# Cross attention and a 32-expert feed-forward layer: the routing weights' way from one row each to 64 rows

## The chip, the cores and the metric

The kernel runs on one core of a Trainium2 chip. The metric is the device time of one execution in microseconds (us). The core has a matrix engine (PE, TensorE), a vector engine (DVE, VectorE), a scalar engine (ACT, ScalarE), GpSimd (POOL) and SyncE (SP), which here only issues DMAs. Each engine runs its own list of instructions in order and waits on semaphores. PE writes to PSUM (8 banks of 128 partitions x 512 float32); DVE and ACT read and write PSUM and SBUF; POOL and the DMAs reach SBUF but not PSUM.

## What is computed

Four batches of 256 tokens, 128 channels. One layer of self and cross attention, then a feed-forward layer (FFN) with a shared expert and 32 routed experts, of which each token uses the best 8. The part that the change touches:

```python
x = hidden_states.reshape(T, h)                       # T = 1024 tokens, h = 128
aff = jax.nn.sigmoid(jnp.dot(x, Wr) + br)             # 32 experts
top_v, top_i = jax.lax.top_k(aff, 8)
top_w = top_v / (jnp.sum(top_v, axis=-1, keepdims=True) + 1e-09)
w_full = jnp.zeros((T, 32)).at[jnp.arange(T)[:, None], top_i].set(top_w)
gate = silu(jnp.einsum('th,ehi->eti', x, Wg) + bg[:, None, :])   # i = 64
up = jnp.einsum('th,ehi->eti', x, Wu) + bu[:, None, :]
down = jnp.einsum('eti,eih->eth', gate * up, Wd) + bd[:, None, :]
routed = jnp.einsum('te,eth->th', w_full, down)
```

## The kernel before

**Attention.** The attention runs in 16 steps (4 batches x 4 groups of 4 heads). In step i, PE computes score tiles (`natural`, `scores`), the probabilities times the values of step i-1 (`attend_self`, `attend_context`, into PSUM bank 6, `B_OUT`), and transposes the output of step i-2 (`turn_out`, into bank 7, `B_MISC`). DVE divides that output by its denominator (`normalize`). Bank 7 is also used by the "tail" of each batch: `y_turn`, `project`, `x2_turn`, `router`, `route_turn`. `take_misc` makes PE wait, before it writes bank 7 again, for whoever reads it. The tails of batches 0 and 1 stand in the steps 6 to 15, those of batches 2 and 3 beside the first items of the FFN (`pe_beside`, `act_beside`, `v_beside`).

**FFN.** Tokens lie along the free dimension in two chunks of 512. Two experts of 64 inner rows make one unit of 128 rows; unit 16 is the shared expert. An item is one unit and one chunk: `WORK` has 34 items, 32 of them routed. The items 0 to 11 are chunk 0, item 12 is the first of chunk 1. Float32 precision is kept by splitting each operand in a rounded upper half (`_hi`) and the rest (`_lo`), so that each product is three matmuls (`product3`). For each routed item:

1. PE: `project_gate` (3 matmuls, bank 0 or 1), the up projection (3 matmuls, bank 2 or 3), and `spread_routes` (1 matmul, L1687, bank 4 or 5): it multiplies the transposed routing weights `routeT` with a 0/1 matrix `spread`, so that the weight of each of the two experts stands in 64 rows.
2. ACT: silu of the gate into `gate` in SBUF (L925).
3. DVE: `gated` = (up + bias) * gate (L1300), then `hid` = gated * the spread weights in PSUM (L1312).
4. ACT rounds `hid` to `hid_hi` (L934); the lower half `hid_lo` is made by POOL for the items 0 to 11 and 31 (L707) and by DVE for the others (L974).
5. PE: the down projection of item n-2 (3 matmuls), added up in bank 6 or 7.

`spread` is made by POOL (`make_spread`) and copied by ACT during the attention steps. The weights of the units are loaded by SP (`load_unit`, three DMAs of 64 KB each, a ring of 6 slots) and split by ACT (L814) and POOL (L638). SP's list is: all loads up to unit 16, then the three stores of the result.

The routing weights of batch b are made by DVE (`router`, `top`, `weights`), transposed by PE (`route_turn`, L1611) and copied to `routeT` by ACT (L834). Chunk c needs the batches 2c and 2c+1.

Of the kernel before, what the change touches and what calls it, by code (L numbers as in the profile page):

```python
# [6 lines left out]
F32R = mybir.dt.float32r  # L7
# [25 lines left out]
SPREADS = 4  # L33
SPREAD_UNITS = 4
# [33 lines left out]
B_GATE, B_UP, B_WIDE = 0, 2, 4  # L68
# [8 lines left out]
def build(nc, x, ctx, w, out):  # L77

    with ExitStack() as stack:
# [17 lines left out]
        spread = sb("spread", [P, PAIRS, P], F32R)  # L97
# [49 lines left out]
        top = sb("top", [P, 2, TOP])  # L147
# [4 lines left out]
        routeT = sb("routeT", [P, TOKENS], F32R)  # L152


        with ExitStack() as attention:
# [8 lines left out]
            spread_f = sb("spread_f", [P, SPREAD_UNITS, P], until=attention)  # L164
# [26 lines left out]
        in_ffn = [sem(f"in_ffn{k}") for k in range(SLOTS)]  # L191
        placed_k = [[sem(f"placed_k{k}_{g}") for g in range(GROUPS)] for k in range(2)]
# [14 lines left out]
        have_spread = sem("have_spread")  # L207
# [54 lines left out]
        spread_copied = sem("spread_copied")  # L262
# [34 lines left out]
        m_wide = sem("m_wide")  # L297
# [26 lines left out]
        for b in range(BATCH - 2):  # L324
            for n, name in enumerate(TAIL):
                tail_at.setdefault(4 * b + 6 + n, []).append((name, b))
            between_at[4 * b + 8] = [("norm", b)]
        late_at[11] = [("route_turn", 0)]
# [11 lines left out]
                     (5, "C"): [("route_turn", 2), ("x2_turn", 3)],  # L340
                     (6, "C"): [("router", 3)],
                     (LEAD - 2, "B"): [("route_turn", 3)]}
# [3 lines left out]
                      (5, "C"): [("route_turn", 2), ("x2_turn", 3)],  # L346
                      (7, "B"): [("router", 3)],
                      (LEAD - 2, "B"): [("route_turn", 3)]}
# [7 lines left out]
                    (6, "A"): [("x2_turn", 3)],  # L356
                    (6, "C"): [("router", 3)],
                    (7, "C"): [("top", 3)],
                    (8, "C"): [("weights", 3)]}
# [5 lines left out]
        POOL_LO = [*range(LEAD), LAST_ITEM - 2]  # L365
# [20 lines left out]
        def turned_bank(i):  # L386

            return {STEPS - 4: B_NAT0, STEPS - 3: B_NATC, STEPS - 2: B_NAT1 + 1, STEPS - 1: B_OUT}.get(i, B_MISC)
# [9 lines left out]
        def lo_done(n):  # L398

            if n in POOL_LO:  # L400
                return pool_lo_done, POOL_LO.index(n) + 1
            return hid_lo_done, VECTOR_LO.index(n) + 1

# [89 lines left out]
        def _(sp):  # L493
# [40 lines left out]
            sp.dma_start(b_down[2 * EXPERTS:2 * EXPERTS + 1, :], row(w["bd_s"])).then_inc(in_down_bias, 16)  # L534
# [15 lines left out]
        def _(pool):  # L550
# [1219 lines left out]
```

## Time and profile before

| | us |
|---|---|
| median of 3 runs | 206.8 (205.07, 206.80, 206.99) |
| the profiled execution, its own time | 204.82 |
| its span in the profile | 203.1 |

So 1.7 us of the profiled execution lie outside its span. Over the span the engines are busy as follows.

| engine | busy us | share |
|---|---|---|
| PE | 188.8 | 93% |
| DVE | 162.2 | 80% |
| ACT | 135.7 | 67% |
| POOL | 98.1 | 48% |

The attention takes the first 107 us or so, the FFN the rest. In the profile a row of the timeline gives the start, the duration, the engine, the source line, the operation, output and inputs, and in brackets the idle time before it and what ended it. Successive matmuls overlap, so that the distance of their starts is what each costs. The share of a DMA queue is the time that its packets took, as a share of 16 DMA engines over the stretch asked for; so share x 16 x stretch is the sum of the packets' durations.

### The profile page before, as it was taken

The page shows a single profiled execution, that of the slowest core. Times are in us where ns is not written, and L with a number is a line of the kernel's source. Part 1 is how long each engine was busy: PE and PEld are TensorE (multiplying, and loading weights), DVE is VectorE, ACT ScalarE, POOL GpSimd, SP SyncE. Part 2 cuts the span into 40 slices and gives each one's busy share as a digit, 9 for nine tenths or more (in the row PEclk, how much of TensorE's full clock was granted, in tenths as well). Part 3 has the DMA queues.
Part 4 walks back from the last instruction along what each step waited for, and adds up shares of the span by engine and source line. Part 5 has one row for each costly group of instructions (what it writes and reads, how often), then busy time and mean ns, then how long its engine had stood idle before and what let it go on. Part 6 is the DMA issues. An engine that isn't in the chain of part 4 may idle for free.

```text
span 203.1 us, 3982 instructions
## 1 busy us (share of the span) xinstructions
PE 188.8 (93%) x1237; PEld 138.5 (68%) x1249; DVE 162.2 (80%) x375; ACT 135.7 (67%) x272; POOL 98.1 (48%) x154
## 2 busy tenths in 40 slices
PE   7968999999999996999999898798999999999993
PEld 2636677777777675777675775686688887887662
DVE  2899998677788959986594899899677879887982
ACT  3447898787898888789779444653655556555571
POOL 7799982243554856259355486683522331000020
PEclk9999999999999999999999999999999999999998
DMA  4355433233343334201301112120000000000003
GB/s 114 96 137 143 106 77 86 49 76 83 74 118 74 75 86 97 65 0 42 75 6 39 38 39 55 34 52 0 3 0 3 0 2 0 0 0 0 3 0 103
DMA packets 20434, 10.40 MB, mean 51 GB/s; under 512 B 11881, under 2 KB 18542, under 8 KB 20414
## 3 DMA queue, kind: packets, MB, share of 16 engines
q1 hardware_dynamic: 19290, 9.24, 18.4%
q0 software_dynamic: 672, 0.69, 1.4%
q10 hardware_dynamic: 452, 0.23, 0.5%
q8 instruction: 10, 0.16, 0.3%
q14 instruction: 10, 0.08, 0.1%
HBM read 4.51 MB, written 0.52 MB: 25 GB/s over the span
## 4 chain that ended last, share of the span: by engine, by line
PE 65%; DVE 18%; issue 6%; ACT 5%; POOL 3%; DMA 1%; DVEq 0%; POOLq 0%
PE psum L1356 10%; PE psum L1358 9%; PE psum L1357 9%; PE psum L1459 6%; PE psum L1515 5%; PE psum L1550 4%; PE psum L1538 4%; PE psum L1520 3%; PE psum L1562 3%; DVE gated L1300 2%; POOL hid_lo L707 2%; PE psum L1458 2%; PE psum L1687 2%; PE psum L1524 2%; PE psum L1543 2%
## 5 line engine op out<-in xcount | busy, mean ns | idle before, releaser
L925 ACT ACTIVATE gate<-psum,bias_cols 128x512 f32<-128x512 f32 (+2 forms) x35 | 23.5, 675 | 30.1 <-PE psum L1358 30.1
L802 ACT ACTIVATE probs<-psum 128x512 f32<-128x512 f32 x64 | 36.3, 597 | 2.1 <-PE psum L1520 1.0
L707 POOL TENSOR_TENSOR hid_lo<-hid,hid_hi 128x512 fp32r<-128x512 f32 x13 | 16.8, 1291 | 32.9 <-ACT hid_hi L934 30.6
L1300 DVE SCALAR_TENSOR_TENSOR gated<-psum,bias_cols,gate 128x512 f32<-128x512 f32 x32 | 24.0, 749 | 10.3 <-ACT gate L925 9.3
L934 ACT CAST hid_hi<-hid 128x512 fp32r<-128x512 f32 (+1 forms) x33 | 20.2, 614 | 7.5 <-DVE hid L1312 6.8
L1459 PE MATMUL psum<-key_blocks,query_rows 96*128 96x512 f32 x48 | 24.1, 544 | 0.0
L1312 DVE TENSOR_TENSOR hid<-gated,psum 128x512 f32<-128x512 f32 x32 | 21.9, 684 | 1.9 <-PE psum L1687 0.2
L638 POOL TENSOR_TENSOR w_late_lo<-w_ffn,w_late_hi 128x384 fp32r<-128x384 f32 x11 | 12.2, 1112 | 18.7 <-ACT w_late_hi L814 18.7
L663 POOL TENSOR_SCALAR_AFFINE_SELECT probs<-probs 128x512 f32<-128x512 f32 x16 | 10.2, 638 | 22.1 <-ACT probs L802 22.0
L1092 DVE TENSOR_REDUCE row_max<-psum 128x4 fp32r<-128x1024 f32 x16 | 19.4, 1215 | 0.0
L1356 PE MATMUL psum<-xT_hi,w_late_hi 128*128 128x512 f32 x42 | 17.0, 404 | 0.0
L1358 PE MATMUL psum<-xT_hi,w_late_lo 128*128 128x512 f32 x42 | 16.6, 394 | 0.0
L1357 PE MATMUL psum<-xT_lo,w_late_hi 128*128 128x512 f32 x42 | 16.5, 392 | 0.0
L1088 DVE TENSOR_REDUCE row_max<-psum 128x4 fp32r<-128x512 f32 x16 | 11.0, 688 | 6.5 <-PE psum L1459 6.5
L974 DVE TENSOR_TENSOR hid_lo<-hid,hid_hi 128x512 fp32r<-128x512 f32 (+2 forms) x22 | 15.2, 696 | 1.1 <-ACT hid_hi L934 0.9
L667 POOL TENSOR_SCALAR_AFFINE_SELECT probs<-probs 128x512 f32<-128x512 f32 x16 | 10.2, 640 | 11.6 <-ACT probs L802 11.6
L809 ACT COPY o_sb<-psum 128x512 f32<-128x512 f32 x16 | 9.4, 587 | 9.5 <-PE psum L1550 9.5
L740 ACT ACTIVATE key_blocks<-key_rows,head_mask 100x256 fp32r<-100x256 f32 x32 | 14.4, 498 | 1.3 <-DMA key_rows<-keys 1.3
L1687 PE MATMUL psum<-routeT,spread 128*128 128x512 f32 x32 | 12.8, 401 | 0.0
L1515 PE MATMUL psum<-query_rows,key_blocks 100*128 100x256 f32 x64 | 11.9, 307 | 0.8 <-DVE queries L1033 0.8
L1515 PEld LDWEIGHTS psum<-query_rows,key_blocks 100*128 100x128 f32 x64 | 8.6, 189 | 5.6 <-issue 4.4
L994 DVE TENSOR_SCALAR key_blocks<-key_rows,head_mask 100x256 fp32r<-100x256 f32 x32 | 11.9, 415 | 0.0
(198 smaller groups left out, 510.5 us busy)
## 6 DMA issues: line engine op xcount, KB each, us to landing
query_rows<-queries SPq DMA_DIRECT2D x46, 64.0 KB, 2.0
key_rows<-keys SPq DMA_DIRECT2D x39, 32.0 KB, 1.9
w_ffn<-in_L_ffn_Wg SPq DMA_DIRECT2D x16, 64.0 KB, 1.9
w_ffn<-in_L_ffn_Wu SPq DMA_DIRECT2D x16, 64.0 KB, 2.2
w_ffn<-in_L_ffn_Wd SPq DMA_DIRECT2D x16, 64.0 KB, 2.1
ckey_rows<-ckeys POOLq DMA_DIRECT2D x12, 32.0 KB, 2.1
key_rows<-keys POOLq DMA_DIRECT2D x9, 32.0 KB, 1.9
x_sb<-in_x SPq DMA_DIRECT2D x2, 128.0 KB, 2.7
```

The costliest lines, as they stand in the source:

```text
L707: pool.tensor_tensor(hid_lo[:, n % 3, :], hid[:, n % 3, :], hid_hi[:, n % 3, :].bitcast(F32), ALU.subtract).then_inc(pool_lo_done, 1)
L802: act.activation(probs[:, i % 2, c, :], bank(B_ST + c % 2), ACT.Exp, scale=SCALE).then_inc(exp_done, 1)
L925: act.activation(gate[rows_of(n), n % 3, part], psum[of, B_GATE + n % 2, part], ACT.Silu, bias=bias_cols[of, BIAS_GATE + u:BIAS_GATE + u + ...
L934: act.copy(hid_hi[rows_of(n - 1), (n - 1) % 3, :], hid[rows_of(n - 1), (n - 1) % 3, :]).then_inc(hid_rounded, 1)
L1092: dve.tensor_reduce(to[:, 1, :], psum[:, B_NAT1:B_NAT1 + 2, :].rearrange("p k (j c) -> p j k c", j=GROUP), AX.XY, ALU.max).then_inc(max_do ...
L1300: dve.scalar_tensor_tensor(out=gated[:, n % 3, :], in0=bank(B_UP + n % 2), scalar=bias_cols[:, BIAS_UP + u:BIAS_UP + u + 1], in1=gate[:, n ...
L1312: dve.tensor_tensor(hid[:, n % 3, :], gated[:, n % 3, :], bank(B_WIDE + n % 2), ALU.mult).then_inc(hid_done, 1)
L1356: pe.matmul(dst, w_hi, x_hi, start=start, stop=False, skip_group_check=True)
L1357: pe.matmul(dst, w_hi, x_lo, start=False, stop=False, skip_group_check=True)
L1358: return pe.matmul(dst, w_lo, x_hi, start=False, stop=stop, skip_group_check=True)
L1459: return pe.matmul(to, query_rows[0:KR, b % 2, g, 0, P * q:P * (q + 1)], blocks[:, :, P * k:P * (k + 1)], start=not diagonal, stop=True, s ...
L1515: ins = pe.matmul(psum[:, to, SEQ * j:SEQ * (j + 1)], key_blocks[0:ROWS, i % RING, 2 * c + j, 0:P], query_rows[0:ROWS, b % 2, g, 0, :], st ...
```

## The change

1. `spread_routes`, `spread`, `make_spread` and ACT's copies of `spread` are removed. Instead the raw routing weights stand in the rows 64 to 95 of `route`, go through the same transpose, and ACT copies them to `route_rows` (SBUF, 32 rows x 1024). For each routed item one DMA on SP reads two rows of it, each 64 times, into one of four slots of `wide` (128 x 512 float32, 256 KB). The slot is written again once the item that used it has its `gated`.
2. ACT's silu writes back into the gate's PSUM bank; the gate has three banks (0, 1, 4). `gated` is now that bank times `wide`, and `hid` is (up + bias) * gated.
3. POOL makes the lower halves of the items 0 to 31.
4. The intermediate tiles of the routers of batches 2 and 3 lie in PSUM bank 5.
5. `turn_out` goes to bank 6 instead of 7, and `attend_self` waits for DVE's `normalized`. The router of batch 0 is finished by DVE in step 10 (before: 9), its weights in step 11 (before: 10), `route_turn` of batch 0 moves from step 11 to 12; `route_turn` 2 and the tail of batch 3 stand one item later.
6. `load_unit` of the units 11 to 16 stands between the new DMAs in SP's list.

```diff
+            for n, (u, c) in enumerate(WORK):
+                if n == 1:
+                    load_unit(sp, SLOTS + 5)
+                if LEAD // 2 <= n < LEAD // 2 + UNITS - LEAD:
+                    load_unit(sp, LEAD // 2 + n)
+                if u == SHARED:
+                    continue
+                r = routed(n)
+                if u == 0:
+                    sp.wait_ge(route_rows_ready, 2 * c + 2)
+                if r >= WIDE_SLOTS:
+                    sp.wait_ge(gated_done, r - WIDE_SLOTS + 1)
+                sp.dma_start(wide[:, r % WIDE_SLOTS, :],
+                             route_rows[RAW + 2 * u:RAW + 2 * u + 2, c * CHUNK:(c + 1) * CHUNK].unsqueeze(1)
+                             .to_broadcast([2, INNER, CHUNK])).then_inc(in_wide_route[r % WIDE_SLOTS], 16)
...
                 if name == "route_turn":
                     act.wait_ge(t_route, b + 1)
+                    act.copy(route_rows[RAW:ONES, tokens(b)], psum[RAW:ONES, B_MISC, 0:SEQ]).then_inc(route_rows_ready, 1)
                     act.copy(routeT[:, tokens(b)], bank(B_MISC, SEQ)).then_inc(routeT_ready, 1)
...
-                        act.activation(gate[rows_of(n), n % 3, part], psum[of, B_GATE + n % 2, part], ACT.Silu,
+                        to = gate[INNER:P, n % 3, part] if u == SHARED else gate_bank(n)
+                        act.activation(to, gate_bank(n)[of, part], ACT.Silu,
...
                 if u != SHARED:
-                    dve.wait_ge(m_up, routed(n + 1))
                     dve.wait_ge(gate_done, n + 1)
-                    dve.scalar_tensor_tensor(out=gated[:, n % 3, :], in0=bank(B_UP + n % 2),
-                                             scalar=bias_cols[:, BIAS_UP + u:BIAS_UP + u + 1],
-                                             in1=gate[:, n % 3, :], op0=ALU.add, op1=ALU.mult).then_inc(gated_done, 1)
+                    dve.wait_ge(in_wide_route[routed(n) % WIDE_SLOTS], 16 * (routed(n) // WIDE_SLOTS + 1))
+                    dve.tensor_tensor(gated[:, n % 3, :], gate_bank(n), wide[:, routed(n) % WIDE_SLOTS, :],
+                                      ALU.mult).then_inc(gated_done, 1)
...
-        POOL_LO = [*range(LEAD), LAST_ITEM - 2]
+        POOL_LO = [*range(LAST_ITEM - 1)]
...
+                if 1 <= i < STEPS - 3:
+                    pe.wait_ge(normalized, i)
...
-                if to == B_MISC:
-                    take_misc(normalized, i + 1)
...
-                if i != STEPS - 3:
-                    for name, b in tail_at.get(i, ()):
-                        tail_rest(name, b)
+                if i == 10:
+                    tail_rest("router", 0)
+                for name, b in tail_at.get(i, ()):
+                    if name != "router":
+                        tail_rest(name, b)
```

Two places show how the instructions move. First SP's list, from the loads of the last units (three rows for each unit) to its end. Before:

```order
L487 DMA w_ffn<-in_L_ffn_Wg 128x2x64
L487 DMA w_ffn<-in_L_ffn_Wu 128x2x64
L489 DMA w_ffn<-in_L_ffn_Wd 128x128
L482 DMA w_ffn<-in_L_ffn_Wg_s 128x64
L483 DMA w_ffn<-in_L_ffn_Wu_s 128x64
L484 DMA w_ffn<-in_L_ffn_Wd_s 64x128
L546 DMA out_x<-result 128x4x128
L546 DMA out_x<-result 128x2x128 x2
```

The same place in the change, where `wide` is a slot for one item's spread weights and `route_rows` the 32 rows they are read from:

```order
L568 DMA wide<-route_rows 128x1x512
L499 DMA w_ffn<-in_L_ffn_Wg 128x2x64
L499 DMA w_ffn<-in_L_ffn_Wu 128x2x64
L501 DMA w_ffn<-in_L_ffn_Wd 128x128
L568 DMA wide<-route_rows 128x1x512
L494 DMA w_ffn<-in_L_ffn_Wg_s 128x64
L495 DMA w_ffn<-in_L_ffn_Wu_s 128x64
L496 DMA w_ffn<-in_L_ffn_Wd_s 64x128
L568 DMA wide<-route_rows 128x1x512 x22
L574 DMA out_x<-result 128x4x128
L574 DMA out_x<-result 128x2x128 x2
```

There are 32 DMAs to `wide`, and the last 22 of them stand in SP's list with no load between them. Second, PE's list in one routed item of chunk 1: gate, up, spread and the down projection of two items before. Before:

```order
L1356 MATMUL psum<-xT_hi,w_ffn_hi 128x512
L1357 MATMUL psum<-xT_lo,w_ffn_hi 128x512
L1358 MATMUL psum<-xT_hi,w_ffn_lo 128x512
L1356 MATMUL psum<-xT_hi,w_ffn_hi 128x512
L1357 MATMUL psum<-xT_lo,w_ffn_hi 128x512
L1358 MATMUL psum<-xT_hi,w_ffn_lo 128x512
L1687 MATMUL psum<-routeT,spread 128x512
L1356 MATMUL psum<-hid_hi,w_late_hi 128x512
L1357 MATMUL psum<-hid_lo,w_late_hi 128x512
L1358 MATMUL psum<-hid_hi,w_late_lo 128x512
```

In the change (the lines of `product3` are 1359 to 1361 there):

```order
L1359 MATMUL psum<-xT_hi,w_ffn_hi 128x512
L1360 MATMUL psum<-xT_lo,w_ffn_hi 128x512
L1361 MATMUL psum<-xT_hi,w_ffn_lo 128x512
L1359 MATMUL psum<-xT_hi,w_ffn_hi 128x512
L1360 MATMUL psum<-xT_lo,w_ffn_hi 128x512
L1361 MATMUL psum<-xT_hi,w_ffn_lo 128x512
L1359 MATMUL psum<-hid_hi,w_late_hi 128x512
L1360 MATMUL psum<-hid_lo,w_late_hi 128x512
L1361 MATMUL psum<-hid_hi,w_late_lo 128x512
```

Ten matmuls an item became nine; nothing else moved in these rows.

## Rows read from the trace of the kernel before

**Rows 1.** Busy time by stage: us, busy (x count) per engine, PEclk, DMA share, GB/s

```profile
107.00:130.00 23.00, 19.48 (x110) 14.36 (x109) 18.18 (x46) 13.07 (x27) 13.54 (x16) 1.00 0.18 44
130.00:144.00 14.00, 13.10 (x60) 10.15 (x59) 12.51 (x28) 7.85 (x16) 8.89 (x8) 1.00 0.09 21
144.00:187.00 43.00, 42.60 (x182) 33.96 (x183) 34.67 (x52) 23.69 (x42) 8.96 (x8) 1.00 0.00 1
```

**Rows 2.** Timeline of PE: the spread matmul of two successive items

```profile
153.93 0.39 PE L1687 MATMUL psum<-routeT,spread 128*128 128x512 f32 x1
154.16 0.40 PE L1356 MATMUL psum<-hid_hi,w_ffn_hi 128*128 128x512 f32 x1
...
156.26 0.39 PE L1687 MATMUL psum<-routeT,spread 128*128 128x512 f32 x1
```

**Rows 3.** Waits from 130 to 203 us: who for whom, us, times, longest

```profile
ACT gate L925 <- PE psum L1358: 23.4, 25, 1.6
```

**Rows 4.** Timeline of DVE: small operations of the routers of batches 2 and 3

```profile
115.49 0.29 DVE L1170 TENSOR_SCALAR logits<-logits 128x64 f32<-128x64 f32 x1
...
132.08 1.05 DVE L1170 TENSOR_SCALAR logits<-logits 128x64 f32<-128x64 f32 x1
...
139.06 0.23 DVE L1207 TENSOR_TENSOR affinity<-affinity,r_top 128x64 f32<-128x64 f32 x1
139.32 1.16 DVE L1214 CAST route<-affinity 128x64 fp32r<-128x64 f32 x1
```

**Rows 5.** Timeline of PE in step 10: `y_turn` of batch 1

```profile
80.75 0.44 PE L1586 MATMUL psum<-ident,y_nat 128*128 128x128 f32 x2 [1.65 <-DVE o_norm L1127]
```

**Rows 6.** The page's costliest groups: POOL's lower halves and weight splits

```profile
L707 POOL TENSOR_TENSOR hid_lo<-hid,hid_hi 128x512 fp32r<-128x512 f32 x13 | 16.8, 1291 | 32.9 <-ACT hid_hi L934 30.6
L638 POOL TENSOR_TENSOR w_late_lo<-w_ffn,w_late_hi 128x384 fp32r<-128x384 f32 x11 | 12.2, 1112 | 18.7 <-ACT w_late_hi L814 18.7
```

**Rows 7.** DMA issues of the whole span: count, KB each, median us to landing

```profile
query_rows<-queries SPq DMA_DIRECT2D x46, 64.0 KB, 2.0
query_rows<-queries ACTq DMA_DIRECT2D x2, 64.0 KB, 2.4
ctx_sb<-in_ctx ACTq DMA_DIRECT2D x1, 64.0 KB, 2.6
w_ctx<-in_L_xattn_Wck ACTq DMA_DIRECT2D x1, 32.0 KB, 3.0
qkc_bias<-in_L_xattn_bq ACTq DMA_DIRECT2D x1, 0.5 KB
qkc_bias<-in_L_xattn_bcq ACTq DMA_DIRECT2D x1, 0.5 KB
```

**Rows 8.** The page's queue of ACT's DMAs: packets, MB, share of 16 engines

```profile
q10 hardware_dynamic: 452, 0.23, 0.5%
```

**Rows 9.** DMA packets from 70.79 to 71.25 us: one 64 KB DMA

```profile
DMA packets 48, 0.07 MB, mean 143 GB/s; under 512 B 16, under 2 KB 16, under 8 KB 48
```

**Rows 10.** The same DMA's queue, packets that start from 70.94 to 71.02 us

```profile
q1 hardware_dynamic: 11, 0.02, 129.6%
```

**Rows 11.** The same, from 71.15 to 71.16 us: its last long packet

```profile
q1 hardware_dynamic: 1, 0.00, 54.4%
```

**Rows 12.** The queue of SP's DMAs, 107 to 200 us (unit loads, first store)

```profile
q1 hardware_dynamic: 4795, 1.43, 6.3%
```

**Rows 13.** Timeline of ACT: the transposed weights of batch 1 are copied

```profile
107.59 0.39 ACT L834 CAST routeT<-psum 128x256 fp32r<-128x256 f32 x1
```

**Rows 14.** Timeline of DVE: `gated` of item 0 and of item 32, the last routed

```profile
110.18 0.75 DVE L1300 SCALAR_TENSOR_TENSOR gated<-psum,bias_cols,gate 128x512 f32<-128x512 f32 x1 [0.65 <-ACT gate L925]
...
193.74 0.75 DVE L1300 SCALAR_TENSOR_TENSOR gated<-psum,bias_cols,gate 128x512 f32<-128x512 f32 x1 [0.42 <-ACT gate L925]
```

More of the change, by code:

```diff
@@ L96, in build @@
         head_mask = sb("head_mask", [P, GROUP])
-        spread = sb("spread", [P, PAIRS, P], F32R)
+        wide = sb("wide", [P, WIDE_SLOTS, CHUNK])
         x_sb = sb("x_sb", [P, TILES, C])
@@ L152, in build @@
         routeT = sb("routeT", [P, TOKENS], F32R)
+        route_rows = sb("route_rows", [P, TOKENS])
         with ExitStack() as attention:
@@ L191, in build @@
         in_ffn = [sem(f"in_ffn{k}") for k in range(SLOTS)]
+        in_wide_route = [sem(f"in_wide_route{k}") for k in range(WIDE_SLOTS)]
         placed_k = [[sem(f"placed_k{k}_{g}") for g in range(GROUPS)] for k in range(2)]
@@ L296, in build @@
         m_up = sem("m_up")
-        m_wide = sem("m_wide")
         m_down = sem("m_down")
@@ L355, in build @@
                     (4, "C"): [("norm", 3)],
[L356 to L359, printed above, removed]
+                    (7, "A"): [("x2_turn", 3)],
+                    (7, "C"): [("router", 3)],
+                    (8, "C"): [("top", 3)],
+                    (9, "C"): [("weights", 3)]}
         RSTD_ITEM = 4
         LAST_ITEM = ITEMS - 1
-        POOL_LO = [*range(LEAD), LAST_ITEM - 2]
+        POOL_LO = [*range(LAST_ITEM - 1)]
         VECTOR_LO = [n for n in range(LAST_ITEM) if n not in POOL_LO]
@@ L402, in lo_done, with gate_bank, affinity_of @@
             return hid_lo_done, VECTOR_LO.index(n) + 1
+        def gate_bank(n):
+            return bank(B_GATES[n % len(B_GATES)])
+        side = bank(B_SIDE, 6 * EXPERTS).rearrange("p (n t e) -> p n t e", n=3, t=2)
+        side_sigmoid, side_affinity, side_logits = side[:, 0, :, :], side[:, 1, :, :], side[:, 2, :, :]
+        def affinity_of(b):
+            return affinity[:, :, :] if b < 2 else side_affinity
         def routed(n):
@@ L682, in _ @@
                     add_bp(i // 2 - 1)
-                if i < BATCH:
-                    pass
-                elif i % 2 and i // 2 - 2 < SPREADS:
-                    make_spread(i // 2 - 2)
                 if ROUND_STEP <= i < STEPS - 1:
@@ L717, in _ @@
                     split_unit(ROUND_AT[n + 1])
-            for u in range(LEAD, UNITS):
-                split_unit(u)
-            lower_half(POOL_LO[-1])
         @block.scalar
@@ L871, in _ @@
                     round_unit(i - ROUND_STEP)
-                if i % 2 and 0 <= i // 2 - 3 < SPREADS:
-                    k = i // 2 - 3
-                    act.wait_ge(have_spread, k + 1)
-                    act.copy(spread[:, SPREAD_UNITS * k:SPREAD_UNITS * (k + 1), :],
-                             spread_f[:, :, :]).then_inc(spread_copied, 1)
                 if i:
@@ L1309, in _ @@
                 if u != SHARED:
-                    dve.wait_ge(m_wide, routed(n + 1))
+                    dve.wait_ge(m_up, routed(n + 1))
                     dve.wait_ge(gated_done, routed(n + 1))
-                    dve.tensor_tensor(hid[:, n % 3, :], gated[:, n % 3, :], bank(B_WIDE + n % 2),
-                                      ALU.mult).then_inc(hid_done, 1)
+                    dve.scalar_tensor_tensor(out=hid[:, n % 3, :], in0=bank(B_UP + n % 2),
+                                             scalar=bias_cols[:, BIAS_UP + u:BIAS_UP + u + 1],
+                                             in1=gated[:, n % 3, :], op0=ALU.add, op1=ALU.mult).then_inc(hid_done, 1)
                 else:
```

125 lines of the change are left out of this document (50 added, 75 removed).

## Prediction

> **What bounds the kernel now.** I read the page, then busy time by stage, then PE's timeline of one item, then the waits, and last the DMA packets. By stage, from 144 to 187 us PE is busy 42.60 of 43 us and DVE 34.67 [rows 1]: the FFN's second half is bound by PE. One item there lasts 156.26 - 153.93 = 2.33 us for ten matmuls, 0.23 us each [rows 2]. ACT waits for the gate's last matmul 25 times, 23.4 us in sum [rows 3], so nobody else is late. From 107 to 144 us PE is busy 32.6 of 37 us and DVE 30.7 [rows 1]: there the routers of batches 2 and 3 stand in DVE's queue, and PE sometimes waits. DMAs are nearly idle from 144 us on (0.00 of 16 engines [rows 1]). The change puts a new transfer of 256 KB per item exactly there, and makes `gated` of each routed item wait for it. So the question is not what PE saves but how long one such transfer takes: it is hidden only if the DMAs bring one each 2.1 us.
>
> **What it removes.** One matmul of ten per item: 0.23 us x 21 routed items of the PE-bound stretch = 4.9 us. In step 10, PE waited 1.65 us for DVE's `o_norm` before `y_turn` [rows 5]; DVE was late because it finished the router of batch 0 first, which now stands behind: 1.65 us gone. DVE's small operations that met POOL took about 1 us in place of 0.2 to 0.3: L1170 took 1.05 us once and 0.29 us once, L1214 1.16 us beside L1207's 0.23 [rows 4]. In PSUM they should take the short time; I saw six such long ones, at most 5 us, and take 3, as PE covers part. POOL's `make_spread` and ACT's copies lie beside PE's attention work: nothing.
>
> **What it adds on the engines.** ACT's silu, DVE's `gated` and `hid` only change their operands: same count, same size, nothing. The new copy to `route_rows` (four, 0.4 us each, as [rows 13]) lies beside PE. `attend_self` waits for `normalized`, which PE waited for in the tail steps anyway: nothing to 0.1 us a step. POOL gets 1.29 us each item, plus 1.11 us for a weight split at some [rows 6]; the five splits of chunk 1 make 2.4 us, over the 2.1 us of an item, so 0.3 us late each, which PE sees at most as 2 us. If item time is set by something slower, all of this and all of PE's saving is worth nothing.
>
> **What one transfer takes.** No row shows this DMA. Its nearest is the 64 KB DMA `query_rows<-queries`: 32 rows of 2 KB, from SBUF to SBUF [rows 7]. It has 48 packets, 32 of 2 KB and 16 of under 512 B [rows 9]: one closing packet for each of 16 DMA engines. A DMA of one row behaves otherwise. ACT's queue issued two of the 64 KB ones (96 packets), one of 128 rows with two pieces each (256 + 16), one of 64 rows (64 + 16), and two of one row [rows 7]. The queue counts 452 packets [rows 8]; 96 + 272 + 80 leaves 4, so each one-row DMA had one data packet and one closing packet: one engine. The number of engines follows the shape. The new DMA's source has two rows at its head (each read 64 times), so I take two engines, with 64 packets of 2 KB each, against 8 for sixteen.
>
> A 2 KB packet costs between two values. Alone, at the end of the query DMA: 54.4% x 16 x 0.01 us = 0.087 us [rows 11]. In its middle, with all engines reading, each pair of them in neighbouring rows: 129.6% x 16 x 0.08 us / 11 = 0.151 us [rows 10]; two such packets in 0.151 us are 27 GB/s for a pair. The new DMA's two engines read two neighbouring rows all the time, so I take 0.151 us: 64 x 0.151 = 9.66 us per transfer; the low end is 64 x 0.087 = 5.6 us. If neighbouring rows are what slows, sixteen engines on these two rows would not be faster than 256 KB at 27 GB/s either: again 9.7 us.
>
> The Trainium skill, page "DMA: Bandwidth & Descriptors", section "Why a DMA increments its semaphore by 16 and not by 1", says that a DMA runs on the largest number of engines up to 16 that divides the slowest dimension above size 1 of both access patterns. Here those are 2 and 128, so it gives two engines; the one-row count above agrees, and no run yet shows two. Its page "SBUF — State Buffer", section "Door 1: The DMA port swizzle", puts four neighbouring partitions on one DMA port and gives 27.2 GB/s for a port; by that figure a transfer is estimated at 262144 B / 27.2 GB/s = 9.6 us, and the trace's crowded price agrees.
>
> With four slots the next transfers are queued, so they follow each other without a gap, and an item takes one transfer.
>
> **The sum.** The weights of batch 1 are ready at 107.98 us [rows 13], less the 1.65 us of step 10: 106.3. From issue to landing a 64 KB DMA takes 2.0 us [rows 7], of which 0.45 us is its packets [rows 9]: 1.55 fixed, 107.9. Then 32 transfers x 9.66 = 309.1: the last lands at 417.0. From `gated` of item 32 to the end of the span before were 203.1 - 193.74 = 9.4 us [rows 14]: 426.4. Outside the span lie 204.8 - 203.1 = 1.7: 428.1. The loads of the units 11 to 16 stand between them; SP's packets of that stretch held each engine 6.3% x 93 us = 5.9 us at most [rows 12], partly while the other engine gains; I take 2. That is 430 us, against 204.8 for the profiled execution, which is 1.0% below the median of 206.8. The other savings are hidden, because DVE waits for the transfer in each item.
>
> What is queued behind that wait: DVE's `hid`, then the weights of batches 2 and 3, so `route_turn` and chunk 1's transfers. Those weights stand behind the items 4 and 9, and four transfers (up to 38 us) are still queued then, more than the few us they take: no gap.
>
> **The rivals.**
>
> *Two engines, not disturbing each other.* For it: most of 0.151 may come from crowding on the written side, which two engines writing far apart halves don't have. Against it: reading neighbours is the one thing that they surely share. Time: 107.9 + 32 x 5.6 + 9.4 + 1.7 + 2 = 300 us. Values between are open. 25% (from 290 to 415).
>
> *The transfer is spread over 16 engines and hidden, so the change does what it says (faster).* Mechanism: 128 packets over 16 engines are 8 x 0.151 = 1.2 us, below 2.1 us an item. It decides wherever a transfer takes under 2.1 us. For it: every DMA of 16 rows or more in this trace reaches that rate. Against it: the one-row DMAs, and the shared source rows. Time: 204.8 - 4.9 - 1.65 - 3 + 2 = 197 us; item 0's `gated`, at 110.18 before [rows 14], would wait until 107.9 + 1.2, so no loss. 12%.
>
> *Hidden, but the gain is eaten.* POOL's 1.29 us after ACT's rounding lengthens the way from gate to down projection, and PE waits instead of multiplying. 4.9 us saved, 3 to 5 us given back: 203 to 206 us. For it: POOL's lower halves are the longest operation in the way [rows 6]; against it: PE works two items ahead. 3%.
>
> *Slower still.* If the packets read from one row line up worse than 0.151 us, or the DMA is split on one engine: above 445 us. 5%.
>
> **How the numbers follow.** The main forecast, 9.66 us per transfer give or take 0.5 (415 to 445 us), has 55%. The range must hold 8 in 10: 55% and the 25% of the faster two-engine case, so 290 to 445 us. The sides: about 1% is what a measurement can tell. Faster 13%, within 1% 2%, slower 85%: the first rival is slower as well, the second is faster, the third is shared.
>
> **What would show it.** In the changed profile: 32 issues of `wide<-route_rows` with 256 KB each, and 130 packets per transfer if two engines carry it, 144 if sixteen do; a distance of 9.7 us between successive `gated`, each ended by the DMA; PE busy under half of the FFN; the DMA share near 2/16 = 0.12 from 108 us to the end; GB/s near 27. `y_turn` of batch 1 should lose its wait of 1.65 us. Wrong would be: `gated` released by ACT, an item of 2.1 us, or a DMA share near 1 for short bursts. A distance of 5.6 us would say that the engines were counted rightly and the packet was mis-sized.

## The result and the profile after

The changed kernel takes 421.0 us (median of 4 runs, 419.8 to 421.4) against 206.0 us before (205.1 to 207.0). The ratio is 2.047, with an interval of 2.037 to 2.057. Forecast were 430 us, range 290 to 445. The profiled execution took 419.8 us, of which 418.1 us are its span. Here and below a time is the median of all executions of a kernel, and a ratio leaves out the few that ran more than 1.5% longer than the fastest at a lower granted clock.

The page of the kernel after, beside the rows of before:

```profile
span 418.1 us, 3900 instructions
PE 249.3 (60%) x1205; PEld 165.5 (40%) x1217; DVE 147.0 (35%) x356; ACT 135.0 (32%) x272; POOL 113.4 (27%) x162
PE   7799999979636563365344464644435464443724
PEclk9999999999955665566666656655656556566855
DMA  3632343311111111111111111111111111111101
GB/s 102 142 85 69 72 98 80 94 33 40 44 33 26 25 30 42 47 44 48 36 29 30 25 31 26 33 26 31 33 25 32 25 34 25 32 28 34 36 23 50
DMA 61%; PE 20%; SPq 8%; DVE 5%; issue 2%; POOL 2%; ACT 1%; DVEq 0%; POOLq 0%; ACTq 0%
L1303 DVE TENSOR_TENSOR gated<-psum,wide 128x512 f32<-128x512 f32 x32 | 22.1, 691 | 237.2 <-DMA wide<-route_rows 237.2
wide<-route_rows SPq DMA_DIRECT2D x32, 256.0 KB
```

The first quarter of the span, the attention, takes as long as it did (the weights of batch 1 are copied at 107.59 us in both). From the first item on, everything waits: `gated` stood 237.2 us in 32 waits, each time for `wide<-route_rows`. The transfers alone make 61% of the chain that ended last. Note that no queue looks full: the DMA share is one tenth and the rate about 30 GB/s. PE is busy about half the time, and its granted clock falls to 0.5 or 0.6 as soon as it waits in each item (before, it was 1.00 from 107 to 187 us). 0.50 is the lower of its two levels, 1.2 GHz; a figure between 0.5 and 1 is the mean of a stretch that holds both.

Busy time of each engine in three stretches (columns: stretch, length, PE, its loads, DVE, ACT and POOL with instruction counts, granted clock, DMA share, GB/s), to be set beside [rows 1]:

```profile
107.00:144.00 37.00, 16.64 (x71) 11.79 (x70) 8.28 (x24) 9.23 (x19) 7.74 (x10) 0.64 0.16 35
144.00:187.00 43.00, 22.27 (x59) 15.59 (x59) 9.70 (x24) 8.33 (x16) 10.81 (x11) 0.58 0.18 40
200.00:300.00 100.00, 48.60 (x101) 29.70 (x102) 17.90 (x36) 14.95 (x27) 16.89 (x14) 0.62 0.13 29
```

A share of 0.13 is two of sixteen engines, as forecast (2/16 = 0.125). What follows is DVE's timeline of five successive `gated` (the bracket: idle time before it, and what ended it), where [rows 14] shows two of before:

```profile
294.55 0.69 DVE L1303 TENSOR_TENSOR gated<-psum,wide 128x512 f32<-128x512 f32 x1 [8.45 <-DMA wide<-route_rows]
302.68 0.69 DVE L1303 TENSOR_TENSOR gated<-psum,wide 128x512 f32<-128x512 f32 x1 [6.56 <-DMA wide<-route_rows]
312.65 0.69 DVE L1303 TENSOR_TENSOR gated<-psum,wide 128x512 f32<-128x512 f32 x1 [8.40 <-DMA wide<-route_rows]
320.65 0.69 DVE L1303 TENSOR_TENSOR gated<-psum,wide 128x512 f32<-128x512 f32 x1 [6.43 <-DMA wide<-route_rows]
330.66 0.69 DVE L1303 TENSOR_TENSOR gated<-psum,wide 128x512 f32<-128x512 f32 x1 [8.43 <-DMA wide<-route_rows]
```

The distances are 8.13, 9.97, 8.00 and 10.01 us. That alternation was not forecast, and it is the key to the mechanism. The DMA packets that start in two stretches of 2 us, each with the queue's packets, MB and share of 16 engines; the first is 296 to 298 us, the second 300.2 to 302.2 us:

```profile
DMA packets 25, 0.05 MB, mean 26 GB/s; under 512 B 0, under 2 KB 0, under 8 KB 25
q1 hardware_dynamic: 25, 0.05, 12.6%
...
DMA packets 49, 0.10 MB, mean 50 GB/s; under 512 B 0, under 2 KB 0, under 8 KB 49
q1 hardware_dynamic: 49, 0.10, 13.0%
```

With the same two engines, a packet of 2 KB takes 12.6% x 16 x 2 us / 25 = 0.161 us in the first and 13.0% x 16 x 2 / 49 = 0.085 us in the second. Both of the prediction's prices (0.151 and 0.087) exist, by turns. The rate by slices of 0.44 us from 293.5 to 311 us shows when:

```profile
GB/s 23 23 28 23 23 28 28 19 28 28 42 23 28 19 28 52 51 47 51 52 47 37 28 19 28 28 19 28 28 23 23 28 23 23 28 28 23 23 28 28
DMA packets 255, 0.52 MB, mean 30 GB/s; under 512 B 4, under 2 KB 4, under 8 KB 254
```

The fast stretch lasts from about 300.1 to 302.7 us. The closing packets, 4 in these 17.5 us, that is two per transfer, mark its borders: one lies between 300.0 and 300.2 us and one between 302.1 and 302.3 us, about 0.5 us before the rate falls. At the first, the engine that is ahead goes from the rows of unit 7 to those of unit 8; at the second, the engine behind does the same, 2.1 us later. Unit 7's rows are 78 and 79, unit 8's 80 and 81. So the packets are fast while one engine reads from the rows 76 to 79 and the other from 80 to 83; with both in one group of four they are slow.

Is it the group, or only that the two engines are at different units? The closing packets of the transfer before lie between 289.5 and 289.7 us and between 294.0 and 294.2 us, so that in between one engine reads unit 7 (rows 78 and 79) and the other still unit 6 (76 and 77): different units, one group. The packets from 290 to 292 us:

```profile
DMA packets 24, 0.05 MB, mean 25 GB/s; under 512 B 0, under 2 KB 0, under 8 KB 24
q1 hardware_dynamic: 24, 0.05, 11.9%
```

They are slow (11.9% x 16 x 2 / 24 = 0.159 us), so it is the group. Two units share a group, hence 10 and 8 us in turn. The alternation needs a distance between the engines, and that grows: among the first ten `gated` the distances are all near 10 us (9.3 to 10.4, 9.98 in the mean, 120.10 to 209.95 us), and near the end those with a change of group, or with one engine alone, take 6.7 us (383.64 to 390.33 and 400.43 to 407.14 us). The distance of the two closing packets, which is what one engine is behind while both are slow, went from 3.4 us (216.5 and 219.9 us) to 7.4 us (392.7 and 400.0 us). What sets the engines apart stays open. Which of the two is ahead at which row I inferred from the closing packets; `rows16apart`, where the two never share a group, tests the rule of the groups without that inference.

### The profile page after: what moved, and what is told of

The parts are those of the page before. It is cut to its first block, busy times and chain, and to the rows that moved or that the text cites. A ratio compares the mean times of both kernels' runs of the same rounds, so it can differ in the third digit from the quotient of the medians.

```text
span 418.1 us, 3900 instructions
## 1 busy us (share of the span) xinstructions
PE 249.3 (60%) x1205; PEld 165.5 (40%) x1217; DVE 147.0 (35%) x356; ACT 135.0 (32%) x272; POOL 113.4 (27%) x162
## 4 chain that ended last, share of the span: by engine, by line
DMA 61%; PE 20%; SPq 8%; DVE 5%; issue 2%; POOL 2%; ACT 1%; DVEq 0%; POOLq 0%; ACTq 0%
DMA wide<-route_rows 61%; SPq L499 3%; PE psum L1462 3%; PE psum L1518 2%; PE psum L1543 2%; PE psum L1555 2%; SPq L568 2%; PE psum L1523 1%; SPq L501 1%; PE psum L1565 1%; PE psum L1461 1%; PE psum L1527 1%; PE psum L1504 1%; PE psum L1484 1%; PE psum L1359 1%
## 5 line engine op out<-in xcount | busy, mean ns | idle before, releaser
L1303 DVE TENSOR_TENSOR gated<-psum,wide 128x512 f32<-128x512 f32 x32 | 22.1, 691 | 237.2 <-DMA wide<-route_rows 237.2
L717 POOL TENSOR_TENSOR hid_lo<-hid,hid_hi 128x512 fp32r<-128x512 f32 x32 | 40.7, 1272 | 219.3 <-ACT hid_hi L933 211.8
L1359 PEld LDWEIGHTS psum<-xT_hi,w_late_hi 128*128 128x128 f32 x42 | 12.6, 299 | 80.1 <-DVE hid L1314 77.7
L1359 PE MATMUL psum<-xT_hi,w_ffn_hi 128*128 128x512 f32 x24 | 16.0, 669 | 41.8 <-DVE hid L1314 30.5
L1359 PE MATMUL psum<-hid_hi,w_late_hi 128*128 128x512 f32 (+2 forms) x23 | 16.9, 736 | 26.0 <-POOL hid_lo L717 22.1
L924 ACT ACTIVATE psum<-psum,bias_cols 128x512 f32<-128x512 f32 x32 | 21.0, 657 | 17.6 <-PE psum L1361 17.6
L1314 DVE SCALAR_TENSOR_TENSOR hid<-psum,bias_cols,gated 128x512 f32<-128x512 f32 x32 | 24.0, 750 | 4.2
L676 POOL TENSOR_SCALAR_AFFINE_SELECT probs<-probs 128x512 f32<-128x512 f32 x16 | 10.2, 637 | 27.3 <-ACT probs L809 27.2
L1361 PEld LDWEIGHTS psum<-xT_hi,w_late_lo 128*128 128x128 f32 x42 | 12.9, 307 | 3.7
L1360 PEld LDWEIGHTS psum<-xT_lo,w_late_hi 128*128 128x128 f32 x42 | 13.1, 312 | 2.1
L1360 PE MATMUL psum<-xT_lo,w_ffn_hi 128*128 128x512 f32 x24 | 13.9, 580 | 0.0
```

Of the source, the lines that this page charges most:

```text
L717: pool.tensor_tensor(hid_lo[:, n % 3, :], hid[:, n % 3, :], hid_hi[:, n % 3, :].bitcast(F32), ALU.subtract).then_inc(pool_lo_done, 1)
L924: act.activation(to, gate_bank(n)[of, part], ACT.Silu, bias=bias_cols[of, BIAS_GATE + u:BIAS_GATE + u + 1]).then_inc(gate_done, 1)
L1303: dve.tensor_tensor(gated[:, n % 3, :], gate_bank(n), wide[:, routed(n) % WIDE_SLOTS, :], ALU.mult).then_inc(gated_done, 1)
L1314: dve.scalar_tensor_tensor(out=hid[:, n % 3, :], in0=bank(B_UP + n % 2), scalar=bias_cols[:, BIAS_UP + u:BIAS_UP + u + 1], in1=gated[:, n ...
L1359: pe.matmul(dst, w_hi, x_hi, start=start, stop=False, skip_group_check=True)
L1360: pe.matmul(dst, w_hi, x_lo, start=False, stop=False, skip_group_check=True)
```

## Experiments

**What a transfer takes.** Four kernels. `rows16apart` keeps the two weight rows of an item 16 rows apart:

```diff
-                    dve.tensor_copy(to[:, :, RAW:ONES], of)
+                    dve.tensor_copy(to[:, :, RAW:ONES].rearrange("p t (h u) -> p t u h", h=2),
+                                    of.rearrange("p t (u h) -> p t u h", h=2))
...
-                             route_rows[RAW + 2 * u:RAW + 2 * u + 2, c * CHUNK:(c + 1) * CHUNK].unsqueeze(1)
+                             route_rows[RAW + u:RAW + u + PAIRS + 1:PAIRS, c * CHUNK:(c + 1) * CHUNK].unsqueeze(1)
```

> The two weight rows of an item are kept 16 rows apart (64 + u and 80 + u) and not side by side; the DMA is otherwise the same, two engines with 64 packets of 2 KB each. Theory (two engines that read from one group of four neighbouring rows share about 26 GB/s; in the changed kernel their packets took 0.16 us nearly always and 0.08 us only in stretches where one engine had moved on to the next group of four): the packet takes 0.08 us always, a transfer 64 x 0.08 = 5.15 us, an item 5.2 to 5.5 us, so the first gated at about 115 us, then 31 x 5.3 = 164, then 11 us of tail and 1.7 outside: 292 us (280 to 300). Rival (the crowding is on the written side, or lies in the two engines themselves): the packet stays at 0.16 us and the time at 420 us.

Measured: 295.4 us, ratio to before 1.438 (1.429 to 1.447), in the theory's range. Three successive `gated` in its DVE timeline, and its packets from 220 to 222 us:

```profile
219.46 0.69 DVE L1304 TENSOR_TENSOR gated<-psum,wide 128x512 f32<-128x512 f32 x1 [3.71 <-DMA wide<-route_rows]
224.73 0.69 DVE L1304 TENSOR_TENSOR gated<-psum,wide 128x512 f32<-128x512 f32 x1 [3.70 <-DMA wide<-route_rows]
230.01 0.69 DVE L1304 TENSOR_TENSOR gated<-psum,wide 128x512 f32<-128x512 f32 x1 [3.70 <-DMA wide<-route_rows]
...
DMA packets 48, 0.10 MB, mean 49 GB/s; under 512 B 0, under 2 KB 0, under 8 KB 48
q1 hardware_dynamic: 48, 0.10, 12.9%
```

The distance is 5.27 us, and from 171 us on nearly all are (up to 171 us, with unit loads between the transfers, they are 5.2 to 6.0 us); the alternation is gone. Engines, packets, bytes and destination are those of the changed kernel; only the source rows moved, and 125.6 us went away. The written side is ruled out as the cause of the slow packet.

`engines16` makes two DMAs of each transfer, one per weight row:

```diff
-                sp.dma_start(wide[:, r % WIDE_SLOTS, :],
-                             route_rows[RAW + 2 * u:RAW + 2 * u + 2, c * CHUNK:(c + 1) * CHUNK].unsqueeze(1)
-                             .to_broadcast([2, INNER, CHUNK])).then_inc(in_wide_route[r % WIDE_SLOTS], 16)
+                for e in range(2):
+                    sp.dma_start(wide[INNER * e:INNER * (e + 1), r % WIDE_SLOTS, :],
+                                 route_rows[RAW + 2 * u + e:RAW + 2 * u + e + 1, c * CHUNK:(c + 1) * CHUNK].unsqueeze(1)
+                                 .to_broadcast([1, INNER, CHUNK])).then_inc(in_wide_route[r % WIDE_SLOTS], 16)
```

> Each transfer is made as two DMAs of 128 KB, one per weight row, whose read side has 64 as its first size above 1, so that 16 engines should carry it (80 packets per DMA with the closing ones, 160 per item). Theory (the read side's group of four rows is a second limit behind the engine count): all engines read one row, 128 packets x 0.079 us = 10.1 us per item, no gain: 118 + 31 x 10.1 + 11 + 1.7 = 444 us (420 to 455), and each packet takes over 1 us. Rival (only the count of engines limits): 8 packets of 0.16 us per engine, 1.3 us per item, hidden, 197 to 202 us.

Measured: 391.3 us, ratio 1.903 (1.893 to 1.913). Its packets from 220 to 260 us:

```profile
DMA packets 770, 1.28 MB, mean 32 GB/s; under 512 B 151, under 2 KB 151, under 8 KB 768
q1 hardware_dynamic: 768, 1.26, 86.9%
```

Sixteen engines at a share of 87% move 32 GB/s, where two at a share of 13% moved 29. A packet took 86.9% x 16 x 40 / 768 = 0.72 us in the mean, closing packets included, against 0.16 us with two engines. So more engines alone give little (391 against 421 us) when all read one group of rows, and an engine counts as busy while its packet waits. I had expected 444 us, over 1 us for each packet, and items 10.1 us apart. The last 19 items came 7.9 us apart (228.45 to 378.72 us), most of them about 9.7 and 6.4 us in turn. In the long distances a packet passes every 9.7 / 128 = 0.076 us, much as with two engines (0.161 / 2 = 0.080): as if a group of rows had one rate, however many engines read it. The short ones fit engines that are spread over two units as above, which I did not check packet by packet. The rival's 197 to 202 us is ruled out either way.

`through_dram` stores the 32 rows of a chunk to DRAM once and spreads them from there:

```diff
+                    sp.dma_start(rows_dram[:, c * CHUNK:(c + 1) * CHUNK],
+                                 route_rows[RAW:ONES, c * CHUNK:(c + 1) * CHUNK]).then_inc(in_rows_dram, 16)
+                    sp.wait_ge(in_rows_dram, 16 * (c + 1))
...
+                                 rows_dram[2 * u + e:2 * u + e + 1, c * CHUNK:(c + 1) * CHUNK].to_broadcast([INNER, CHUNK])
```

> The 32 weight rows of a chunk are first stored to a scratch tensor in DRAM (one DMA of 64 KB), and each item's 256 KB are spread from there by two DMAs of 128 KB on 16 engines. Theory (with 16 engines and no shared read rows in SBUF the transfer fits under the 2.1 us of an item): 128 packets on 16 engines are 8 x 0.09 to 0.16 = 0.7 to 1.3 us per item, hidden; the first item waits for the store and the load, 2 + 2 + 1 us, about 113 us in place of 110; 200 to 206 us. Rival 1 (reading one DRAM row many times is slow: in the kernel before, a bias row read 128 times for b_wide took 4.1 us to land against 2.1 us for a weight of the same size, so 2 us more for 128 packets): an item takes 2 to 4 us, 210 to 260 us. Rival 2 (what limits is the written side): 420 us.

Measured: 210.3 us, ratio 1.023 (1.017 to 1.029). Its DMA issues, its packets from 170 to 180 us, and the only two `gated` that waited more than 0.3 us for a transfer:

```profile
wide<-rows_dram SPq DMA_DIRECT2D x64, 128.0 KB, 2.9
rows_dram<-route_rows SPq DMA_DIRECT2D x2, 64.0 KB, 1.6
...
DMA packets 754, 1.26 MB, mean 126 GB/s; under 512 B 145, under 2 KB 145, under 8 KB 752
q1 hardware_dynamic: 752, 1.24, 42.2%
...
113.89 0.69 DVE L1309 TENSOR_TENSOR gated<-psum,wide 128x512 f32<-128x512 f32 x1 [4.10 <-DMA wide<-rows_dram]
154.35 0.69 DVE L1309 TENSOR_TENSOR gated<-psum,wide 128x512 f32<-128x512 f32 x1 [4.75 <-DMA wide<-rows_dram]
```

The transfers are now hidden except at the first items of each chunk: of the loss of 215 us, all but 4 went with their source in SBUF. Against `engines16`, which splits each transfer in the same way, only the source differs: 391 and 210 us. The time is above the theory's 200 to 206 us. What remains is 3.7 us at item 0 (110.18 before [rows 14]), 4.75 us at item 12, and something in the pace of the items, below. What the change saves elsewhere sets these off in part, so that they need not add up to 4. By its time (210 to 260 us) rival 1, a DRAM row read many times is slow, would fit; by its mechanism it does not: a packet took 42.2% x 16 x 10 / 752 = 0.09 us, and at 126 GB/s the transfers kept up with items that wait for other things.

`four_transfers` leaves out all but the first four:

> Only the first four transfers are made, and the later items multiply by what lies in the four slots, so the weights of 28 of 32 items are wrong ones: the changed kernel's compute without its transfers. Theory (all the loss is the transfers, and PE bounds what is left at nine matmuls per item): the first four items still come 9 to 10 us apart (last one landed at about 150 us against 117 us of the kernel before), then 28 items of 2.1 us = 59, then 10 us of tail: 220 us, which is 197 us were the first four transfers free; item distance late in the FFN 2.1 us. Rival (GpSimd's lower halves of 1.29 us after ACT's rounding set the item's pace): item distance over 2.3 us, 226 us or more.

Measured: 231.6 us, ratio 1.124 (1.117 to 1.131), over 11 us above the theory and in the rival's range. The fourth item came at 152.63 us, the last at 220.97. The late distances are 2.06 and 2.24 us in turn, 2.16 in the mean, so the rival's pace (over 2.3) is not met, though what it names is real: with the lower halves on DVE the same items take 2.04 us (`dram_old_pool`, below). Most of the miss is in my sum: items 4 to 12 still have the routers of batches 2 and 3 among them and took 2.7 us each, (176.69 - 152.63) / 9, and the shared unit of chunk 0 takes an item's time too. I had counted 28 items of 2.1 us. The kernel shows only time: most of its items multiply by another item's weights.

**What the other parts are worth.** `before_dve_order` is the kernel before with DVE's new order of step 10 alone, `before_order_bank` has the new bank and wait of `attend_self` as well:

```diff
-        late_at[11] = [("route_turn", 0)]
+        late_at[12] = [("route_turn", 0)]
...
+                if i == 10:
+                    tail_rest("router", 0)
...
+                if 1 <= i < STEPS - 3:
+                    pe.wait_ge(normalized, i)
```

> The kernel before with one part of the change alone: DVE does the router of batch 0 behind the o_norm and the residual of its step, and the weights of batch 0 (and their transposes) one step later; banks and waits stay. Theory (the prediction's step: PE's 1.65 us before y_turn is gone and nothing comes in its place): 206.0 - 1.65 = 204.4 us. Rival (DVE has the same work in the same steps, and PE meets it a step later): 206 us, with new idle time of PE between 80 and 100 us.

> The same as before_dve_order and also the other part of that edit: the turned-out heads go to the bank of the attention's output and not to the bank shared by the tails, so attend_self of step i waits until DVE has normalized step i - 1. Theory (in the changed kernel PE stood 1.20 us at 84.96 us and 1.23 us at 91.43 us before attend_self, each time until just after an o_norm): the 1.65 us are gained and 2.4 us are given back, 206 to 207 us, that is 1.5 to 2.5 us above before_dve_order. Rival (the prediction's: this wait costs nothing to 0.1 us a step): the same time as before_dve_order, 204.4 us.

Measured: `before_dve_order` 207.1 us, ratio 1.0065 (1.003 to 1.010); `before_order_bank` 205.7 us, ratio 0.999 (0.996 to 1.002); before 205.5 us in this comparison. In `before_dve_order` `y_turn` no longer waits, but the list of PE's waits from 70 to 108 us has a new one in its place:

```profile
PE psum L1358 <- DVE o_norm L1127: 1.7, 1, 1.7
```

It stands at 85.92 us, one step behind the old one at 80.75 [rows 5]: the wait for DVE moved and kept its size. Behind it the granted clock fell: 0.69 from 85.3 to 90 us and 0.95 from 90 to 95 us, where the kernel before and `before_order_bank` have 1.00. At these shares PE loses 0.31 x 4.7 + 0.05 x 5 = 1.7 us by estimate, and the transposes of the weights of batch 1 came 1.7 us later, at 108.12 us against 106.40 before. The rival was right. With the new bank they came at 106.27. There, and in the changed kernel, PE stands at `attend_self` instead, twice, 2.4 us in sum. PE's timeline of the changed kernel, and DVE's `o_norm` just before:

```profile
84.96 0.62 PE L1543 MATMUL psum<-probs,value 128*9 128x256 f32 x8 [1.20 <-issue]
91.43 0.62 PE L1543 MATMUL psum<-probs,value 128*9 128x256 f32 x8 [1.23 <-issue]
...
84.57 0.29 DVE L1126 TENSOR_TENSOR o_norm<-psum,r_den 128x128 f32<-128x128 f32 x1
91.04 0.29 DVE L1126 TENSOR_TENSOR o_norm<-psum,r_den 128x128 f32<-128x128 f32 x1
```

Both matmuls start 0.1 us after the end of `o_norm`, though the profile puts the wait down to "issue". This was the theory for `before_order_bank`, and its absolute time (205.7) is near the 206 to 207 expected; but its sign against `before_dve_order` was wrong, because that kernel did not gain its 1.65 us in the first place. Its own two waits of 1.2 us left the clock at 1.00, so the clock accounts for the order of the two kernels in these traces. Why 2.4 us of waits cost no more than the 1.65 us before is not shown.

`dram_sbuf_routers` and `dram_old_pool` undo one part each in `through_dram`:

```diff
-            return affinity[:, :, :] if b < 2 else side_affinity
+            return affinity[:, :, :]
```

```diff
-        POOL_LO = [*range(LAST_ITEM - 1)]
+        POOL_LO = [*range(LEAD), LAST_ITEM - 2]
```

> The kernel whose weights come through DRAM (210.3 us), with the routers of batches 2 and 3 in SBUF as before the change (logits, sigmoid and affinity); the PSUM bank stays unused. Theory (the prediction's 3 us: small operations of DVE take about 1 us in SBUF where they meet GpSimd, 0.2 to 0.3 us in PSUM): 211 to 213 us, and in the trace single small operations of 0.8 to 1.3 us between 118 and 147 us. Rival (the long ones lie beside waits for PE or for the transfers): 210.3 us give or take 0.3, although they are long.

> The kernel whose weights come through DRAM (210.3 us), with the lower halves of hid done as before the change: GpSimd's for items 0 to 11 and the last but two, DVE's (0.69 us) for the others; the five late weight splits follow item 11 on GpSimd. Theory (in the PE-bound stretch items last 2.09 and 2.24 us in turn, 2.17 in the mean, where nine matmuls of 0.232 us are 2.09: the 0.08 us are PE's wait for GpSimd's 1.29 us): items of 2.09 us, 21 x 0.08 = 1.6 us less, 208.7 us. Rival 1 (the 0.08 us are something else): 210.3 us. Rival 2 (DVE gets 0.69 + 0.75 + 0.69 = 2.13 us per item and becomes the bound): items of 2.2 us or more and 211 us or more.

Measured: `dram_sbuf_routers` 214.0 us, ratio 1.035 (1.031 to 1.040) where `through_dram` had 1.023, 1 us above its theory's range; `dram_old_pool` 206.4 us, ratio 1.001 (0.998 to 1.005). Two of the long small operations of the first, in DVE's timeline, and what POOL did meanwhile:

```profile
129.87 1.13 DVE L1216 TENSOR_TENSOR affinity<-affinity,r_top 128x64 f32<-128x64 f32 x1
149.18 1.29 DVE L1221 CAST route<-affinity 128x64 fp32r<-128x64 f32 x1
...
129.62 1.29 POOL L723 TENSOR_TENSOR hid_lo<-hid,hid_hi 128x512 fp32r<-128x512 f32 x1 [0.62 <-ACT hid_hi L939]
149.09 1.32 POOL L723 TENSOR_TENSOR hid_lo<-hid,hid_hi 128x512 fp32r<-128x512 f32 x1 [1.05 <-ACT hid_hi L939]
```

Each starts while a lower half runs on POOL and ends 0.06 to 0.09 us after it (131.00 against 130.91, 150.47 against 150.41), so the small operation waits for POOL's. In PSUM the same two take 0.23 and 0.21 us. The routers' move to PSUM is worth 0.012 x 205.5 = 2.5 us by the ratios, 3.7 by the medians and 4.0 by the spans (212.4 and 208.4). `dram_old_pool` gains more than its theory of 1.6 us: 2.3 us by the spans (208.4 and 206.1), 3.9 by the medians, 4.5 by the ratios. It has POOL's five late weight splits in one row behind item 11, as the kernel before, so the two effects are not told apart. Two successive `gated` of `through_dram`, then of `dram_old_pool`:

```profile
181.32 0.69 DVE L1309 TENSOR_TENSOR gated<-psum,wide 128x512 f32<-128x512 f32 x1 [0.51 <-ACT psum L930]
183.56 0.69 DVE L1309 TENSOR_TENSOR gated<-psum,wide 128x512 f32<-128x512 f32 x1 [0.66 <-ACT psum L930]
```

```profile
180.01 0.69 DVE L1312 TENSOR_TENSOR gated<-psum,wide 128x512 f32<-128x512 f32 x1
182.05 0.69 DVE L1312 TENSOR_TENSOR gated<-psum,wide 128x512 f32<-128x512 f32 x1
```

What PE's weight loads (PEld) wait for in the two kernels, the first from 160 to 200 us, the second from 160 to 197 us (us in total, times, longest):

```profile
PEld psum L1365 <- POOL hid_lo L723: 4.7, 15, 0.8
...
PEld psum L1368 <- DVE hid_lo L982: 1.0, 3, 0.5
```

With GpSimd's lower halves PE meets them in nearly every item, and the items last 2.24 and 2.08 us in turn; with DVE's, from item 17 on, they last 2.04 to 2.10, so that the second rival (DVE becomes the bound, 2.2 us or more) is not met: from item 17 to item 28 `through_dram` needs 189.94 - 166.13 = 23.8 us and `dram_old_pool` 22.6, 1.2 less. The last three items came 4.31, 2.40 and 2.45 us apart with GpSimd's halves and 4.22, 2.11 and 2.04 with DVE's: 0.8 us more. That makes 2.0 of the 2.3 us between the two spans. What the medians show above that lies in no trace that I have.

**A version that beats both.** Two kernels put the better parts together: weights through DRAM, lower halves as before, routers in PSUM, and the router of batch 3 and the transposes of the weights of batches 2 and 3 one item earlier; the second also moves ACT's copy of the weights of batch 1 ahead of two exponentials.

```diff
-                     (LEAD - 1, "B"): [("route_turn", 3)]}
+                     (LEAD - 2, "B"): [("route_turn", 3)]}
```

> dram_old_pool (206.4 us), with the router of batch 3 and the transposes of the weights of batches 2 and 3 one item earlier, where they stood before the change. In dram_old_pool item 12, the first of chunk 1, waited 5.14 us for its transfer, since the weights of batch 3 were copied at 148.5 us. Theory (the way from these weights to the landed transfer, 5.9 us, is what item 12 waits for, and an item is 2.1 to 2.8 us): the wait falls to 2.5 to 3 us, 203.5 to 204.5 us, just under the kernel before (205.5 us). Rival (the earlier router work displaces as much of PE's and DVE's work in items 5 to 10): 206.4 us, the wait shorter and the items before it longer.

> dram_pool_early, and ACT copies the weights of batch 1 ahead of its last two exponentials of the attention (they were ready in PSUM at 106.63 us and copied at 107.59 us). Theory (item 0 waits for its transfer, so it starts by 1 us earlier): 1 us less than dram_pool_early, gated of item 0 at 112.5 us in place of 113.5. Rival (PE's last attention work waits for the exponentials, and x2_turn and the items behind it with it): no gain, or up to 0.7 us lost.

Measured: `dram_pool_early` 202.9 us, ratio 0.987 (0.982 to 0.991): faster than before by 1.3%, a small gain, but its whole interval lies below 1; it is 0.6 us under the theory's range. Item 12 now waits 2.73 us, as expected, and the late matmuls run without a gap at the full clock. Its `gated` of item 12, and its busy time from 144 to 187 us beside [rows 1]:

```profile
151.35 0.69 DVE L1312 TENSOR_TENSOR gated<-psum,wide 128x512 f32<-128x512 f32 x1 [2.73 <-DMA wide<-rows_dram]
...
144.00:187.00 43.00, 42.79 (x184) 33.56 (x183) 37.65 (x58) 28.43 (x48) 9.78 (x9) 1.00 0.41 126
```

`dram_pool_early_copy` has 202.4 us, ratio 0.984 (0.979 to 0.990); the two intervals overlap, so whether the copy's place is worth anything stays open. The trace kept of it does not show whether item 0 came earlier.

## Why the prediction was right, and where it was off

**Which work ends last: right.** Every `gated` of a routed item waits for its transfer, and no other saving is seen. The distance is (407.14 - 120.10) / 31 = 9.26 us.

**Number of engines: right.** Two closing packets per transfer and a share of 0.125. The rule of the Trainium skill, page "DMA: Bandwidth & Descriptors", section "Why a DMA increments its semaphore by 16 and not by 1", gave the same two; this trace agrees.

**Price of a packet: right in kind, off in size by the drift.** I put 0.151 us on all packets, because two engines read neighbouring rows "all the time". They don't: one engine runs ahead, by 3.4 us at 216 us and by 7.4 us at the end, and while the two are in different groups of four rows a packet takes 0.085 us. Packets in one group take 0.161 us, so the error has both signs: 31 x (9.66 - 9.26) = 12.4 us too much. That the forecast was only 9 us off is partly luck: had the engines kept together, at the 9.98 us of the first distances, the sum would have come to 120.1 + 31 x 9.98 + 11.0 + 1.7 = 442 us by estimate, almost at the end of the main forecast (415 to 445 us). The drift, which I did not foresee, took it to the other side. `rows16apart` shows the low end as a kernel of its own: 295 us, where the first rival was put at 300. The Trainium skill, page "SBUF — State Buffer", section "Door 1: The DMA port swizzle", says that four neighbouring partitions share one port; the borders of the fast stretch (78 and 79 against 80 and 81), 26 GB/s within a group and 49 GB/s 16 rows apart agree with it.

**Sixteen engines on two rows would not be faster: right in kind.** It said 9.7 us a transfer again; `engines16` has 8.3 us in the mean ((378.72 - 119.91) / 31) and 391 us.

**The sum, term by term.** First `gated` at 120.10 us, where 107.9 + 9.66 = 117.6 was said: 2.5 too little, of which 1.65 is step 10, which gained nothing (the weights were copied at 107.6 us, not at 106). Of the other 0.85 us about 0.5 is the packet's price: the 128 packets of 2 KB of the first transfer took 0.159 us each, 10.2 us an engine where 9.66 was said. The rest I put down to the unit loads that share the engines, untested. The transfers: 12.4 too much. The tail: 418.1 - 407.14 = 11.0 us against 9.4, 1.6 too little; PE went through it at a granted clock of 0.50 (0.95 from 193 to 203 us before), which I take for the cause. No edit tests it, but the other kernels agree: from the last `gated` to the end `rows16apart` and `engines16` took 10.9 us at 0.50, `through_dram` 9.3 us at 1.00 and `four_transfers` 9.3 us at 0.88. The 2 us for loads are in the first and second terms. 430 + 2.5 - 12.4 + 1.6 - 2 = 419.7, and 419.8 was measured.

**What was hidden and would have been wrong.** Three small terms stood in the sum of the rival at 197 us. The spread matmul's saving showed fully only with DVE's lower halves (2.04 us an item against 2.33; that is 0.29 us, 0.06 more than the 0.23 reckoned, and no run says why). The step of the prediction that fails is "`attend_self` waits for `normalized`, which PE waited for in the tail steps anyway: nothing to 0.1 us a step": PE waited 1.2 us in each of two steps, and the 1.65 us of step 10 were not there to be had. The 3 us for the routers in PSUM were well sized (2.5 to 4.0). GpSimd's lower halves cost 2.3 to 4.5 us, where I gave at most 2 for the splits alone; the mechanism of the third rival was real, and I gave it 3%. None of these terms could show in the 421 us, because every item waits for its transfer.

## What to carry to other kernels

Before a broadcast out of SBUF replaces a matmul, ask two things of its source: how many DMA engines the access pattern gets, and from how many groups of four SBUF rows they read at once; here the first limit alone left the kernel at 1.44 times its old time and the second alone at 1.90, and a detour through DRAM (1.6 us to store, 2.9 us to load) removed both here. A DMA engine's busy share need not tell its speed: 26 and 50 GB/s both showed 0.13, and 0.87 showed 32 GB/s. A wait that an edit removes is gained only if the engine that was late has less to do; here DVE had the same work, and the wait came back one step later with its old size (1.65 and 1.67 us), and behind it the granted clock fell for a while; the kernel came out 0.65% slower.

## What the runs showed of the hardware

- Two DMA engines that read 2 KB packets from one group of four neighbouring SBUF rows take 0.161 us per packet, and 0.085 us from two groups. Different rows of one group are as slow (0.159 us). Sixteen engines that read a unit's two rows, and later those of its neighbour too, move 32 GB/s together.
- Reading one 2 KB row of DRAM 64 times per DMA, with 16 engines, kept up at 126 GB/s.
- Small DVE operations of 128x64 in SBUF that started while POOL's lower half ran took 1.13 and 1.29 us and ended 0.06 to 0.09 us after it; with their operands in PSUM they took 0.23 and 0.21 us.
- PE that waits in each item was granted less clock: 0.58 to 0.64 over the FFN of the changed kernel, 1.00 where it is fed without a gap (`dram_pool_early`, 144 to 187 us). The tail, at 0.50, took 1.6 us longer.
